# Where the later maxima of the keys are kept, and the join of two sets of them

## The chip, the cores and the metric

The kernel runs on one core of a Trainium2 chip. The metric is the device time of one execution in microseconds; smaller is better. Times of the kernel before are the median of three runs. The engines are named as in the profile: PE is TensorE (PEld its weight loads), DVE is VectorE, ACT is ScalarE, POOL is GpSimd, and SP is the engine whose queue issues the DMAs.

## The reference

One transformer block on `x` of 8 batches, 1024 tokens, 256 channels:

```
x = x + layernorm(attention(layernorm(x)))      # 16 heads of 64, causal, softmax
x = x + layernorm(channel_mix(layernorm(x)))    # sigmoid gate, squared ReLU, token shift

# attention, per batch and head
scores = (x Wq)(x Wk)^T / 8 + rel_table[clip(s - t + 16, 0, 32)]
scores = where(s <= t, scores, -inf)
out    = softmax(scores) (x Wv);   out @ Wp + bp
```

The softmax needs, for each query, a bound on its row of scores. The kernel takes the row's maximum of a cheaper product (high halves of q and k only), and the change concerns how those maxima are stored.

## The kernel before, in words

The work goes over 64 pairs of heads (8 batches of 8 pairs). One loop body works on one pair, and at the same time on parts of its neighbours: the projections of a pair two ahead, the maxima of the next pair, the second half of the pair before, and the output projection and channel mix of one block of 128 tokens of an earlier batch. Each engine has its instructions of a body in an order written out by hand; the engines meet at semaphores. There are two banks of PSUM for everything that is not scores (`misc`), two tiles of scores (`score_ps`) and one for the maxima (`max_ps`).

**The maxima.** For the next pair, PE fills `max_ps` nine times (`fill`, f from 0 to 8, L651 and, for the diagonal windows, L660). A query block i of 128 rows (8 in all) has either one reduction or, from i = 4 on, two: one over keys 0 to 511 (not diagonal) or part of them, and one that holds the diagonal. `FILLS` lists what a fill holds. After each fill, DVE reduces it (`maxima`, L1237 for fill 1, L1242 for the others) into `row_max`, a tile of 128 partitions and two planes of 128 floats. Columns in a group of 8 are (head of two, i modulo 4). In plane 0, columns 0 to 7 hold the maxima of the first four blocks, columns 8 to 15 the diagonal ones of the later four, columns 16 to 23 the others of the later four.

**The join.** `join_maxima` (L1249) waits until all nine fills are reduced, and then one reduction over the two groups of 8 in plane 0 writes the 8 final maxima of the later blocks to plane 1. PE transposes plane 0 after the fourth fill (`transpose_maxima`, L671) and plane 1 after the join, at the end of its body. ACT makes a row of shifts out of each transpose (`shift`, L959), and SP sends it to `shift_all`, from which PE adds it to the scores (L633).

**What stands around the join.** On DVE: the bias of tile 11 (`add_bias`, L1258), the join, the statistics of `y` (L1188, L1192), the bias of the next pair's tile 0, `low_probs` 11 (L1226). On PE: score 11, score 0 of the next pair, the transpose of plane 1, and then the next body: the value product of the channel mix (L743), fill 0, score 1, a product of probabilities and values (L694 to L696), the projections q0 and q1 (L585). On POOL, which has its own order: the normalisations (L382 to L399), the last step of the output rows (`final`, L1697), and the low halves of the probabilities for five of the twelve tiles (`low_probs`, L1670). Of these, tiles 8 and 10 come right after `final`. On SP: the rows of the output (L467, behind POOL's `final`), in every second body the values of two pairs (`v_pair`, L433), the store of a chunk (L444), the load of an `o_cur` block (L453), the load of the next `xh` (L463).

Of the kernel before, what the change touches and what calls it, by code (L numbers as in the profile page):

```python
# [35 lines left out]
ALU = mybir.AluOpType  # L36
ACT = mybir.ActivationFunctionType
AX = mybir.AxisListType
# [106 lines left out]
def build(nc, x, wqkv, wp, bp, table, w_r, w_k, w_v, mu_r, mu_k, out):  # L145
    with ExitStack() as ctx:
        def sb(name, shape, dt):
            return ctx.enter_context(nc.sbuf_tensor(name, shape, dt))
# [4 lines left out]
        def sem(name):  # L153
            return ctx.enter_context(nc.semaphore(name))
# [58 lines left out]


        row_max = sb("row_max", [P, 2, P], F32)
        later_max = row_max[:, 0, 8:24].rearrange("p (a h i) -> p a h i", a=2, h=2)
        shift_row = [sb(f"shift_row{c}", [8, P], F16) for c in range(2)]

        probs0 = sb("probs0", [P, 2, 2560], F16)
# [75 lines left out]
        max_ready = sem("max_ready")  # L295
# [36 lines left out]
        def wait(eng, semaphore, value):  # L332

            if isinstance(value, int) and value <= 0:
                return
            eng.wait_ge(semaphore, value)
# [843 lines left out]
        def _(dve):  # L1180
# [47 lines left out]
            def maxima(m, par, ahead, f):  # L1228

                n = 2 * m + par + ahead  # L1230
                dve.wait_ge(filled, NF * n + f + 1)
                if f == 0:
                    wait(dve, full["mt0"], n)
                    wait(dve, full["mt1"], n)
                if f == 1:
                    dst = row_max[:, 0, 0:32].rearrange("p (a b h i) -> p h a b i", a=2, b=2, h=2)[:, :, :, 0, 1:2]
                    last = dve.tensor_reduce(dst, max_ps[:].rearrange("p h (a w) -> p h a w", a=2), AX.X, ALU.max)  # L1237
                else:
                    for i, key, width, col, diagonal in FILLS[f]:
                        dst = (row_max[:, 0, 0:8].rearrange("p (h i) -> p h i", h=2) if i < 4  # L1240
                               else later_max[:, 0 if diagonal else 1])
                        last = dve.tensor_reduce(dst[:, :, i % 4:i % 4 + 1], max_ps[:, :, col:col + width], AX.X,  # L1242
                                                 ALU.max)
                last.then_inc(fill_used, 1)

            def join_maxima(m, par, ahead):
                n = 2 * m + par + ahead
                dve.wait_ge(fill_used, NF * (n + 1))
                dve.tensor_reduce(row_max[:, 1, 0:8], row_max[:, 0, 8:24].rearrange("p (a k) -> p k a", a=2), AX.X,  # L1249
                                  ALU.max).then_inc(max_ready, 1)  # L1250

            def add_bias(m, par, ahead, t, at):
                n = 2 * m + par + ahead
# [188 lines left out]
            for span in ALL_SPANS:  # L1442
                def body(m, par, at, span=span, has=span.has):
# [13 lines left out]
                    if has["next"]:  # L1457
                        maxima(m, par, 1, 0)
# [16 lines left out]
                    if has["next"]:  # L1475
                        maxima(m, par, 1, 1)
# [8 lines left out]
                    if has["next"]:  # L1485
                        maxima(m, par, 1, 2)
# [47 lines left out]
                    if has["next"]:  # L1534
                        join_maxima(m, par, 1)
# [257 lines left out]
```

## Time and profile before

| | |
|---|---|
| median of three runs | 2399.51 us (2395.8 to 2409.04) |
| profiled execution, its time | 2395.8 us |
| its span, first to last instruction | 2394.0 us |
| PE busy | 2221.1 us, 93% of the span |
| DVE busy | 2043.0 us, 85% |
| ACT busy | 1681.4 us, 70% |
| POOL busy | 1498.1 us, 63% |

Busy time is the union of an engine's instructions in the profile. Waits for semaphores, branches and the issuing of DMAs are not in it. Matmuls are pipelined and their ends are modelled, so PE's share is no measure of how near it is to its peak. A releaser is what an engine's idle time ended with, as the semaphores tell.

### The profile page before, as it was taken

The page shows a single profiled execution, that of the slowest core. Times are in us where ns is not written, and L with a number is a line of the kernel's source. Part 1 is how long each engine was busy: PE and PEld are TensorE (multiplying, and loading weights), DVE is VectorE, ACT ScalarE, POOL GpSimd, SP SyncE. Part 2 cuts the span into 40 slices and gives each one's busy share as a digit, 9 for nine tenths or more (in the row PEclk, how much of TensorE's full clock was granted, in tenths as well). Part 3 has the DMA queues.
Part 4 walks back from the last instruction along what each step waited for, and adds up shares of the span by engine and source line. Part 5 has one row for each costly group of instructions (what it writes and reads, how often), then busy time and mean ns, then how long its engine had stood idle before and what let it go on. Part 6 is the DMA issues. An engine that isn't in the chain of part 4 may idle for free.

```text
span 2394.0 us, 75663 instructions
## 1 busy us (share of the span) xinstructions
PE 2221.1 (93%) x30080; PEld 1486.8 (62%) x30080; DVE 2043.0 (85%) x3985; ACT 1681.4 (70%) x2526; POOL 1498.1 (63%) x2594
## 2 busy tenths in 40 slices
PE   3788889999999999999999999999999999999885
PEld 1455556666666666666666666666666666666664
DVE  6788878988888898888888988889898898988856
ACT  2577767777777776777777777777777777777743
POOL 2244335667776766767767777677677767565752
PEclk9999999999999999999999999999999999999997
DMA  6011111122122112212112211211221221121230
GB/s 166 28 41 42 40 48 51 39 68 64 52 65 64 57 42 68 62 50 68 55 39 68 64 57 59 64 57 42 68 63 50 67 62 52 40 64 59 62 108 21
DMA packets 182416, 139.81 MB, mean 58 GB/s; under 512 B 10416, under 2 KB 173104, under 8 KB 182064
## 3 DMA queue, kind: packets, MB, share of 16 engines
q1 hardware_dynamic: 182064, 134.98, 19.1%
q8 instruction: 238, 3.90, 0.7%
q14 instruction: 114, 0.93, 0.1%
HBM read 57.81 MB, written 43.06 MB: 42 GB/s over the span
## 4 chain that ended last, share of the span: by engine, by line
PE 77%; DVE 8%; DMA 6%; SPq 3%; ACT 3%; issue 2%; POOL 1%; DVEq 0%; POOLq 0%; ACTq 0%
PE score_ps L629 13%; PE misc L585 11%; PE misc L600 7%; PE max_ps L651 6%; PE misc L712 6%; PE misc L694 6%; DMA xh<-x 5%; PE misc L696 5%; PE misc L695 5%; PE score_ps L633 4%; PE misc L732 2%; PE misc L706 2%; PE misc L735 2%; PE max_ps L660 2%; DVE probs L1226 1%
## 5 line engine op out<-in xcount | busy, mean ns | idle before, releaser
L1670 POOL TENSOR_TENSOR probs<-probs_f,probs 128x1024 f16<-128x1024 f32 (+1 forms) x320 | 616.7, 1936 | 344.9 <-DVE x_mv L1192 194.5
L1242 DVE TENSOR_REDUCE row_max<-max_ps 128x2 f32<-128x1024 f32 (+2 forms) x640 | 633.0, 1006 | 29.9 <-PE max_ps L660 15.2
L977 ACT ACTIVATE score_ps<-score_ps,score_unit 128x1024 f32<-128x1024 f32 (+3 forms) x448 | 347.9, 777 | 197.9 <-DVE score_ps L1258 150.4
L694 PE MATMUL misc<-v_pair,probs 128*128 128x65 f16 x4608 | 445.3, 195 | 11.3 <-DVE q_lo L1201 7.8
L694 PEld LDWEIGHTS misc<-v_pair,probs 128*128 128x128 f16 x4608 | 418.9, 97 | 46.5 <-issue 36.7
L695 PE MATMUL misc<-v_pair,probs 128*128 128x64 f16 x4608 | 443.9, 194 | 0.0
L696 PE MATMUL misc<-v_pair,probs 128*128 128x65 f16 x4608 | 443.2, 194 | 0.0
L696 PEld LDWEIGHTS misc<-v_pair,probs 128*128 128x128 f16 x4608 | 421.5, 98 | 0.0
L695 PEld LDWEIGHTS misc<-v_pair,probs 128*128 128x128 f16 x4608 | 421.3, 98 | 0.0
L1226 DVE TENSOR_TENSOR probs<-score_ps,probs 128x1024 f16<-128x1024 f32 (+3 forms) x448 | 373.7, 834 | 46.1 <-ACT probs L995 43.4
L585 PE MATMUL misc<-xT,w_split 128*128 128x512 f16 x1536 | 369.6, 385 | 25.6 <-DVE o_stage L1270 16.5
L977 ACT ACTIVATE probs_f<-score_ps,score_unit 128x1024 f32<-128x1024 f32 (+1 forms) x320 | 328.1, 1025 | 54.1 <-PE score_ps L633 36.0
L995 ACT CAST probs<-score_ps 128x1024 f16<-128x1024 f32 (+3 forms) x448 | 317.3, 708 | 12.5
L995 ACT CAST probs<-probs_f 128x1024 f16<-128x1024 f32 (+1 forms) x320 | 307.3, 960 | 4.2
L629 PE MATMUL score_ps<-q_hi,k_hi 64*128 64x512 f16 (+3 forms) x1536 | 253.5, 325 | 37.0 <-DVE probs L1226 35.4
L1258 DVE TENSOR_TENSOR score_ps<-score_ps,bandT 128x288 f32<-128x288 f32 (+2 forms) x576 | 236.0, 420 | 44.5 <-PE score_ps L633 43.9
L585 PEld LDWEIGHTS misc<-xT,w_split 128*128 128x128 f16 x1536 | 140.7, 99 | 203.9 <-issue 44.1
L651 PE MATMUL max_ps<-k_hi,q_hi 64*128 64x512 f16 (+3 forms) x1536 | 225.4, 330 | 35.6 <-DVE row_max L1242 21.7
L633 PE MATMUL score_ps<-shift_all,shift_unit 64*128 64x512 f16 (+3 forms) x1536 | 252.2, 324 | 0.0
L629 PE MATMUL score_ps<-q_lo,k_hi 64*128 64x512 f16 (+3 forms) x1536 | 252.0, 323 | 0.0
L629 PE MATMUL score_ps<-q_hi,k_lo 64*128 64x512 f16 (+3 forms) x1536 | 252.0, 323 | 0.0
L600 PE MATMUL misc<-w_split,xT 128*128 128x256 f16 x1536 | 193.3, 277 | 0.0
(181 smaller groups left out, 4062.8 us busy)
## 6 DMA issues: line engine op xcount, KB each, us to landing
v_pair<-v_calc SPq DMA_DIRECT2D x64, 516.0 KB, 3.7
o_scratch<-o_stage SPq DMA_DIRECT2D x128, 256.0 KB, 2.5
o_cur<-o_scratch SPq DMA_DIRECT2D x56, 512.0 KB, 4.6
xh<-x SPq DMA_DIRECT2D x56, 128.0 KB, 4.1
x_res<-x SPq DMA_DIRECT2D x56, 128.0 KB, 2.1
out<-out_sb SPq DMA_DIRECT2D x56, 128.0 KB, 1.7
shift_all<-shift_row SPq DMA_DIRECT2D x256, 1.0 KB
probs<-wqkv SPq DMA_DIRECT2D x1, 3072.0 KB, 13.2
```

The costliest lines, as they stand in the source:

```text
L585: last = pe.matmul(bank[:], w_split[:, w, which, k, bass.ds(pair, P)], xT[:, a, k, bass.ds(ring + half * 512, 512)], start=step == 0, stop ...
L600: last = pe.matmul(bank[:, i * 2 * P:(i + 1) * 2 * P], xT[:, a, k, bass.ds(ring + (first + i) * P, P)], w_split[:, w, 2, k, bass.ds(pairs, ...
L629: pe.matmul(tile[:, h, 0:width], k_part[rows, ring, keys], q_part[rows, ring, cols], start=step == 0, stop=False)
L651: last = pe.matmul(max_ps[:, h, col:col + width], qk_hi[0][rows, ring, i * P:(i + 1) * P], qk_hi[1][rows, ring, key:key + width], start=Tr ...
L694: pe.matmul(bank[:, at:at + D + 1], high, v_high, start=j == 0, stop=False)
L695: pe.matmul(bank[:, at:at + D], high, v_low, start=False, stop=False)
L696: last = pe.matmul(bank[:, at:at + D + 1], low, v_high, start=False, stop=j == i)
L977: nc.scalar.activation(dst, score_ps[t % 2][:, :, 0:width], ACT.Exp, scale=score_unit[:]).then_inc(exp_done, 1)
L995: nc.scalar.copy(dst, src).then_inc(hi_done, 1)
L1226: dve.tensor_tensor(low, score_ps[t % 2][:, :, 0:width], high, ALU.subtract).then_inc(lo_done_dve, 1)
L1242: last = dve.tensor_reduce(dst[:, :, i % 4:i % 4 + 1], max_ps[:, :, col:col + width], AX.X, ALU.max)
L1670: pool.tensor_tensor(low, copy_of(par + ahead, t)[:, 0:2 * width], high, ALU.subtract).then_inc(lo_done_pool, 1)
```

## The change

The diagonal maxima of the later four blocks go straight to plane 1, columns 0 to 7. Those that are not diagonal go to columns 8 to 15 of plane 0. The join is an element-wise maximum of the two, written over the first of them, in place of a reduction over 16 columns. The waits and the place of each instruction in its engine's order are as before.

```diff
-        later_max = row_max[:, 0, 8:24].rearrange("p (a h i) -> p a h i", a=2, h=2)
+        row_max_a = row_max[:, 0, 8:16].rearrange("p (h i) -> p h i", h=2)
...
                 if f == 1:
-                    dst = row_max[:, 0, 0:32].rearrange("p (a b h i) -> p h a b i", a=2, b=2, h=2)[:, :, :, 0, 1:2]
+                    dst = row_max[:, 0, 0:16].rearrange("p (a h i) -> p h a i", a=2, h=2)[:, :, :, 1:2]
                     last = dve.tensor_reduce(dst, max_ps[:].rearrange("p h (a w) -> p h a w", a=2), AX.X, ALU.max)
                 else:
                     for i, key, width, col, diagonal in FILLS[f]:
-                        dst = (row_max[:, 0, 0:8].rearrange("p (h i) -> p h i", h=2) if i < 4
-                               else later_max[:, 0 if diagonal else 1])
+                        dst = (row_max[:, i // 4, 0:8].rearrange("p (h i) -> p h i", h=2) if diagonal
+                               else row_max_a)
...
             def join_maxima(m, par, ahead):
                 n = 2 * m + par + ahead
                 dve.wait_ge(fill_used, NF * (n + 1))
-                dve.tensor_reduce(row_max[:, 1, 0:8], row_max[:, 0, 8:24].rearrange("p (a k) -> p k a", a=2), AX.X,
-                                  ALU.max).then_inc(max_ready, 1)
+                both = row_max[:, 1, 0:8].rearrange("p (h i) -> p h i", h=2)
+                dve.tensor_tensor(both, both, row_max_a, ALU.max).then_inc(max_ready, 1)
```

## Rows read from the trace of the kernel before

**Rows 1.** The page, busy time by engine, and the chain that ended last.

```profile
PE 2221.1 (93%) x30080; PEld 1486.8 (62%) x30080; DVE 2043.0 (85%) x3985; ACT 1681.4 (70%) x2526; POOL 1498.1 (63%) x2594
...
PE 77%; DVE 8%; DMA 6%; SPq 3%; ACT 3%; issue 2%; POOL 1%; DVEq 0%; POOLq 0%; ACTq 0%
```

**Rows 2.** Stages: length; busy (instructions) of PE, PEld, DVE, ACT, POOL; clock; DMA share, GB/s.

```profile
1223.00:1257.00 34.00, 33.97 (x474) 22.89 (x472) 31.14 (x61) 25.85 (x40) 24.98 (x46) 1.00 0.15 44
1257.00:1293.00 36.00, 34.28 (x472) 22.78 (x470) 31.01 (x61) 25.71 (x40) 24.54 (x45) 1.00 0.24 72
```

**Rows 3.** Timeline around one join: start, us, engine, instruction, [idle <-releaser].

```profile
1222.70 3.25 POOL L1670 TENSOR_TENSOR probs<-probs_f,probs 128x1024 f16<-128x1024 f32 x2
...
1223.03 0.16 DVE L1249 TENSOR_REDUCE row_max<-row_max 128x8 f32<-128x16 f32 x1
...
1223.13 0.38 PE L633 MATMUL score_ps<-shift_all,shift_unit 64*128 64x512 f16 x2
...
1223.44 0.14 PEld L671 LDWEIGHTS max_ps<-ident,row_max 128*128 128x128 f32 x1 [0.42 <-DVE row_max L1249]
```

**Rows 4.** Timeline: five of the 64 joins, POOL's instruction beside three.

```profile
109.58 1.16 POOL L1670 TENSOR_TENSOR probs<-probs_f,probs 128x512 f16<-128x512 f32 x1 [1.49 <-ACT probs L995]
...
110.62 0.16 DVE L1249 TENSOR_REDUCE row_max<-row_max 128x8 f32<-128x16 f32 x1
...
444.85 2.14 POOL L1670 TENSOR_TENSOR probs<-probs_f,probs 128x1024 f16<-128x1024 f32 x1
...
445.20 0.16 DVE L1249 TENSOR_REDUCE row_max<-row_max 128x8 f32<-128x16 f32 x1
...
1257.09 0.16 DVE L1249 TENSOR_REDUCE row_max<-row_max 128x8 f32<-128x16 f32 x1
...
1293.28 0.16 DVE L1249 TENSOR_REDUCE row_max<-row_max 128x8 f32<-128x16 f32 x1
...
2264.02 2.13 POOL L1670 TENSOR_TENSOR probs<-probs_f,probs 128x1024 f16<-128x1024 f32 x1
...
2264.12 0.16 DVE L1249 TENSOR_REDUCE row_max<-row_max 128x8 f32<-128x16 f32 x1
```

**Rows 5.** Timeline of SP's queue and DVE behind the join at 1257 us.

```profile
1256.87 0.35 SPq L467 DMA_DIRECT2D out<-out_sb  x1
...
1263.71 0.42 DVE L1270 TENSOR_TENSOR o_stage<-misc,inv_sum 128x256 f32<-128x256 f32 x1 [1.61 <-DMA o_scratch<-o_stage]
1265.27 0.43 DVE L1188 BATCH_NORM_STATS2 xh_bn<-xh 128x6 f32<-128x256 f32 x1 [1.13 <-DMA xh<-x]
```

**Rows 6.** Waits by name over the run: total us, times, longest.

```profile
DVE xh_bn L1188 <- DMA xh<-x: 44.4, 30, 3.4
...
PEld max_ps L671 <- DVE row_max L1249: 37.6, 64, 1.7
...
DVE o_stage L1270 <- DMA o_scratch<-o_stage: 26.4, 28, 2.2
```

**Rows 7.** Groups by shape: count, busy us, mean ns, idle before, releasers.

```profile
L1670 POOL TENSOR_TENSOR probs<-probs_f,probs 128x1024 f16<-128x1024 f32 x256 | 544.9, 2130 | 326.7 <-DVE x_mv L1192 194.5 <-ACT probs L995 132.1
...
L1242 DVE TENSOR_REDUCE row_max<-max_ps 128x2 f32<-128x1024 f32 x384 | 467.7, 1218 | 16.8 <-PE max_ps L660 5.8 <-PE max_ps L651 4.6
...
L1226 DVE TENSOR_TENSOR probs<-score_ps,probs 128x1024 f16<-128x1024 f32 x128 | 156.1, 1220 | 36.6 <-ACT probs L995 36.5
...
L1249 DVE TENSOR_REDUCE row_max<-row_max 128x8 f32<-128x16 f32 x64 | 10.2, 160 | 0.0
...
L1580 DVE TENSOR_TENSOR xT<-xT 128x4 f32<-128x4 f32 x18 | 2.9, 163 | 0.6
```

**Rows 8.** Timeline of DVE and POOL in the last stretch.

```profile
2327.00 0.16 DVE L1580 TENSOR_TENSOR xT<-xT 128x4 f32<-128x4 f32 x1
...
2329.72 2.78 POOL L1746 TENSOR_TENSOR k_lo<-probs,q_lo 128x256 f32<-128x256 f32 x4 [12.38 <-ACT probs L1119]
```

**Rows 9.** The join's line: ns least/median/greatest, first to last start.

```profile
L1249 DVE TENSOR_REDUCE row_max<-row_max x64: 157/159/164, 78.6 to 2264.1; 128x8 f32<-128x16 f32 x64
```

## The prediction

> **What bounds the kernel now.** I read the page first. The parts by engine [rows 1] name TensorE (PE): busy 2221 of 2394 us, more than any other. VectorE (DVE) has 2043 us, 85%. The chain that ended last is PE for 77%, DVE for 8% and DMA for 6%. Any stall of PE between two matmuls is therefore paid, unless PE would have stood a little later anyway.
>
> The table by stage then sets two neighbouring pairs side by side [rows 2]. Between the joins at 1223 and 1257 us PE is busy for 33.97 of 34.00 us; between those at 1257 and 1293 us for 34.28 of 36.00 us. So there are two sorts of body. I call them tight (34.06 us from join to join, 1223.03 to 1257.09) and loose (36.19 us, 1257.09 to 1293.28) [rows 3, 4]. What makes the second loose is seen in DVE's timeline after 1261 us [rows 5]: its work on `o_stage` waits 1.61 us for the transfer `o_scratch<-o_stage`, then its statistics of `xh` wait 1.13 us for `xh<-x`. The waits by name say that this is regular: 30 waits of 44.4 us for `xh<-x`, 28 of 26.4 us for `o_scratch<-o_stage` [rows 6].
>
> Last I read what stands around the join (L1249). DVE starts it at 1223.03 and takes 0.16 us; PE's weight load for the transpose of the maxima (L671) starts at 1223.44 and has waited for the join alone, while the last matmuls of `score`, begun at 1223.13 and 0.38 us long, run out [rows 3]. Over the run this load waited 37.6 us for the join, in 64 waits [rows 6]. So the join is already as late as PE can bear: each microsecond that it gets later moves L671 and all that is queued behind it on PE (L743, the next pair's fill 0, its scores).
>
> **The change part by part.** *The maxima of the fills.* Nine fills a pair write the same number of maxima as before, with the same shapes; only the columns and the plane differ. Fill 1 keeps its one reduction to 128x4, with a destination stride of 8 floats where it was 16; the others keep theirs to 128x2, 1218 ns for 128x1024 [rows 7]. I take 0. Four of them now write plane 1, which the previous pair's second transpose reads. `maxima` already waits for both transposes of the previous pair at fill 0, so no wait is added, and no instruction, DMA or semaphore is moved.
>
> *The join, own time.* 64 reductions of 128x8 from 128x16, 160 ns each, become 64 `tensor_tensor` of 128x8 from twice 128x8. The nearest row is L1580, also a `tensor_tensor` with both inputs in SBUF, 128x4, 163 ns [rows 7]. That is 64 x 3 ns = 0.2 us more. Below, even a join of no length would give back only the 10.2 us of all 64 [rows 7].
>
> *The join, its company.* The reduction reads one operand from SBUF. The new instruction reads two. In the main loop DVE's two-operand instructions take one operand from PSUM (`score_ps` or `misc`, as L1270 and L1226 in [rows 5, 7]), and those run beside POOL without a mark. Those with two from SBUF stand in the first and the last stretch of the program, and POOL is idle beside them: L1580 and its neighbours from 2327.00 us, for one, while POOL's next work begins at 2329.72 [rows 8]. So the trace does not show such an instruction beside a POOL instruction. But that is what it meets: at 1223.03 POOL is 0.33 us into `low_probs` (L1670), which reads `probs_f` and `probs` from SBUF for 2.13 us [rows 3, 7]. I followed all 64 joins: in 53, from 445.20 us to the last at 2264.12 us, the same POOL instruction had started 0.03 to 0.35 us earlier and had 1.78 to 2.10 us left [rows 3, 4]; of the eleven before, seven met the last 0.12 us of the shorter one (as 110.62 against 109.58 + 1.16) and four nothing [rows 4].
>
> The cost is bounded on one side by no interplay (0.2 us in all) and on the other by waiting until POOL is done. What the rows show of POOL itself is that its two SBUF operands cost it dearly: 2130 ns for 1024 elements is 2.1 ns an element, where DVE takes 1.2 ns with one of its operands from SBUF (L1226, 1220 ns for 1024) [rows 7]. A POOL instruction that reads two operands thus looks bound by its reads, and a new reader of the same memory most likely meets it there. I take the wait, and of its two forms the one until the running instruction ends.
>
> The present join, with its one operand, is not held: 157 to 164 ns in all 64 [rows 9], POOL running beside 60 of them. The Trainium skill, page "SBUF — State Buffer", section "Who interferes with whom", says of this: a reduction never contends, while a VectorE instruction with both inputs in SBUF contends with a GpSimd instruction that reads SBUF, and whichever came second stands still until the first has ended. The trace agrees on the reduction and holds no case of the other. By that rule the change costs the waits that I sum below; without it, 0.2 us. It speaks plainly against the change.
>
> **The sum.** At 1223.03 the join would run from 1224.83 (1222.70 + 2.13) to about 1224.99, 1.80 us late. PE's transpose follows it by what it does now and starts 1.80 us late, and PE has nothing else: its queue is in order. DVE is late as well: the statistics of `y`, the bias of the next pair's tile 0, `low_probs` 11. POOL does not wait for those: it is busy with two `low_probs` until 1225.95 [rows 3].
>
> Tight bodies keep it all. Of the 53 delayed joins 29 open a body of under 34.7 us (or the last one): 29 x 1.89 us (mostly 1.80, ten of them 2.1) = 55 us.
>
> Loose bodies have cover: both transfers are issued in a queue that POOL's `out_sb` released at 1256.87, before the join, so that they land as early as now, and DVE, 1.80 us late, finds 1.61 + 1.13 us of its waiting gone [rows 5]. I take each body's cover as its length less 34.06 us and pay the rest. 24 loose bodies have covers of 0.9 to 4.7 us, 14 of them over 1.8; the others leave 0.3 to 0.9 us each, 6 us together. Seven early joins give 7 x 0.12 = 1 us. Sum: 55 + 6 + 1 = 62 us, with the 0.2 for the instruction itself lost in the rounding.
>
> The profiled execution took 2395.8 us with a span of 2394.0, 1.8 us outside it, and stands 3.7 us under the median of the runs, 2399.5. From its own time: 2395.8 + 62 = 2458; from the median, 2399.5 + 62 = 2462. I predict 2460 us, between the two.
>
> **The rivals.** *No interplay (not slower).* DVE reads both operands beside POOL as it now reads one. For it: the operands are 8 elements each, and no row of this trace shows DVE held by POOL. Against it: the reading rate of POOL above. It decides if the join lasts under 0.2 us while L1670 runs; 2399.5 + 0.2 = 2400 us.
>
> *The cover doesn't hold, or the queue goes against DVE.* If PE's own order, not the two transfers, sets the loose bodies once the join is late, all 53 waits are paid: 53 x 1.87 = 99 us, 2499 us. If DVE also loses the turn at 1224.83 to POOL's second `low_probs`, which follows without a gap and ends at 1225.95, a join is 2.92 us late: 29 x 2.9 = 84, and 23 from the loose bodies after their cover, 2508 us. For it: POOL's two instructions stand back to back [rows 3]. Against it: 1.72 us of PE's idle time in the loose stretch [rows 2].
>
> *The element-wise form is shorter (faster).* The nearest row speaks for 3 ns more, not less, and all 64 joins together are 10.2 us [rows 7]. Even if they were free, that would not reach 0.5%, about 12 us, which is what a measurement of this kernel can tell from no change.
>
> **How the numbers follow.** One wait with cover: 0.60, with its own range 2440 to 2480 us. Waits without cover or for two instructions: 0.19, 2480 to 2515. No interplay: 0.18, 2395 to 2410. Faster by something unseen: 0.03. Slower by over 0.5% is the sum of the first two, 0.79; the same 0.18; faster 0.03. A range for 8 in 10 can't leave out the case of no interplay, since the first two hold only 0.79: it goes from 2397 to 2506 us.
>
> **What would show it.** In the profile after: the join at 64 instructions with a mean near 1.7 us (its end at the end of POOL's first L1670), or its time as idle before it; the wait of PE's L671 for it near 37.6 + 98 = 135 us; the tight bodies at 35.9 us and the loose ones near 36.2; DVE's waits for `xh<-x` and `o_scratch<-o_stage` much under 44.4 and 26.4 us; POOL's L1670 unchanged at 2130 ns. A join of 160 to 170 ns with its start where it was would prove the main step wrong; a join that is late with the loose bodies at 38 us would prove the cover wrong.

## The result, and the profile after

The changed kernel takes 2430.87 us, the median of four runs (2426.18 to 2432.48), against 2397.99 us before in the same comparison. By the means of the runs, from which all ratios below are taken, that is 1.0125 times (1.009 to 1.016, the 95% interval that stands behind each ratio). It is slower by 33 us in the medians (30 in the means), by the mechanism that the prediction named, and by about half of what it summed: 62 us. The 2431 us lie between the prediction's two cases, 2395 to 2410 us for no interplay and 2440 to 2480 for its main one. The wide range of 2397 to 2506 us holds them only because it was stretched from the one over to the other. The profiled execution took 2431.3 us over a span of 2429.5, so 35.5 us more span than before.

The page gives the busy time of the engines and the chain that ended last:

```profile
PE 2216.6 (91%) x30080; PEld 1482.4 (61%) x30080; DVE 2128.2 (88%) x3985; ACT 1694.0 (70%) x2526; POOL 1499.2 (62%) x2594
...
PE 81%; DVE 10%; ACT 2%; DMA 2%; issue 2%; SPq 1%; POOL 1%; DVEq 0%; POOLq 0%; ACTq 0%
PE score_ps L629 13%; PE misc L585 13%; PE misc L600 7%; PE max_ps L651 7%; PE misc L694 6%; PE misc L712 6%; PE misc L695 5%; PE misc L696 5%; PE score_ps L633 4%; DVE row_max L1250 4%; PE misc L732 2%; PE misc L706 2%; PE misc L735 2%; PE
```

Against [rows 1], DVE is busy for 85 us more, and an instruction on 8 elements (L1250) has 4% of the chain. DMA has gone from 6% to 2% of it. Both halves of the result are in these two shares. The line of the join says the first (duration in ns, least, median, greatest; who waited for it, us and times):

```profile
L1250 DVE TENSOR_TENSOR row_max<-row_max x64: 156/1823/2130, 79.7 to 2299.1; 128x8 f32<-128x8 f32 x64
...
  PEld max_ps L671: 118.2, 64
  PE max_ps L671: 86.6, 63
```

In [rows 9] it was 157/159/164. Among the 64, the eleven before 445 us last 0.16 us still, as they meet POOL in its last 0.12 us or not at all. The next 52 last 1.79 to 2.13 us. The last one came when POOL had 0.80 us left and lasts 0.82. The timeline around one join, every engine:

```profile
1194.55 3.24 POOL L1670 TENSOR_TENSOR probs<-probs_f,probs 128x1024 f16<-128x1024 f32 x2
...
1194.88 1.82 DVE L1250 TENSOR_TENSOR row_max<-row_max 128x8 f32<-128x8 f32 x1
...
1194.98 0.38 PE L633 MATMUL score_ps<-shift_all,shift_unit 64*128 64x512 f16 x2
...
1196.75 0.14 PEld L671 LDWEIGHTS max_ps<-ident,row_max 128*128 128x128 f32 x1 [1.89 <-DVE row_max L1250]
1196.75 0.33 PE L671 MATMUL max_ps<-ident,row_max 128*128 128x128 f32 x1 [1.40 <-DVE row_max L1250]
1196.82 0.73 PEld L743 LDWEIGHTS misc<-wv_sb,k_act 128*128 128x128 f32 x4
```

The 3.24 us of POOL's row hold two instructions; the first takes 2.13 us (as it does alone, in a row further down) and so ends at 1196.68; the join ends at 1196.70; PE's transpose starts at 1196.75. POOL's pair of instructions takes 3.24 us, as in [rows 3] (3.25), so it is POOL that is served and DVE that stands. Beside [rows 3], note PE's own row: it now has 1.40 us of idle time. Before, L671 had none at the join of [rows 3]; only its weight load had waited. That holds for 54 of the 64 joins, as the view of the join's line in the kernel before says (who waited for it, us, times):

```profile
  PEld max_ps L671: 37.6, 64
  PE max_ps L671: 9.7, 10
```

The ten are the first ten joins; the trace shows 0.87 to 1.25 us of PE's own idle time at each.

The second half is in the table by stage (length; busy us of PE, PEld, DVE, ACT, POOL; clock; DMA share; GB/s) and in the waits:

```profile
1195.00:1230.50 35.50, 34.07 (x474) 22.87 (x470) 32.90 (x61) 26.15 (x40) 25.06 (x46) 1.00 0.25 73
1230.50:1266.00 35.50, 34.07 (x474) 22.89 (x470) 32.73 (x61) 26.14 (x40) 25.05 (x46) 1.00 0.14 43
```

```profile
DVE xh_bn L1188 <- DMA xh<-x: 17.2, 20, 2.3
```

These two, a loose one first, have become alike: 35.50 us. A tight body pays 1.44 us. A loose one, 36.19 us in [rows 4], is shorter than it was. Of the 21 loose bodies twelve are at 35.5 us now, the other nine at 35.7 to 37.2. The waits for `xh` fell from 44.4 us, and those for the store of `o_stage`, 26.4 us in [rows 6], to 1.3:

```profile
DVE o_stage L1270 <- DMA o_scratch<-o_stage: 1.3, 1, 1.3
```

The table sums the bodies over the whole trace, from join to join. The forecast is what the prediction's own rule gives from the trace of the kernel before, stretch by stretch:

| stretch | before | after | change | forecast |
|---|---|---|---|---|
| start, and the first 11 bodies | 445.2 | 445.6 | +0.4 | +0.8 |
| 21 tight bodies (numbers 11 to 51, odd) | 716.8 | 746.4 | +29.6 | +37.8 |
| 21 loose bodies (12 to 52, even) | 762.4 | 753.6 | -8.8 | +3.5 |
| the last 10 bodies and the end | 469.5 | 483.9 | +14.4 | +19.7 |
| span | 2394.0 | 2429.5 | +35.5 | +61.8 |

### The profile page after: what moved, and what is told of

The parts are those of the page before. It is cut to its first block, busy times and chain, and to the rows that moved or that the text cites. A ratio compares the mean times of both kernels' runs of the same rounds, so it can differ in the third digit from the quotient of the medians.

```text
span 2429.5 us, 75663 instructions
## 1 busy us (share of the span) xinstructions
PE 2216.6 (91%) x30080; PEld 1482.4 (61%) x30080; DVE 2128.2 (88%) x3985; ACT 1694.0 (70%) x2526; POOL 1499.2 (62%) x2594
## 4 chain that ended last, share of the span: by engine, by line
PE 81%; DVE 10%; ACT 2%; DMA 2%; issue 2%; SPq 1%; POOL 1%; DVEq 0%; POOLq 0%; ACTq 0%
PE score_ps L629 13%; PE misc L585 13%; PE misc L600 7%; PE max_ps L651 7%; PE misc L694 6%; PE misc L712 6%; PE misc L695 5%; PE misc L696 5%; PE score_ps L633 4%; DVE row_max L1250 4%; PE misc L732 2%; PE misc L706 2%; PE misc L735 2%; PE max_ps L660 2%; DMA xh<-x 2%
## 5 line engine op out<-in xcount | busy, mean ns | idle before, releaser
L977 ACT ACTIVATE probs_f<-score_ps,score_unit 128x1024 f32<-128x1024 f32 (+1 forms) x320 | 328.1, 1025 | 54.1 <-PE score_ps L633 35.8
L651 PE MATMUL max_ps<-k_hi,q_hi 64*128 64x512 f16 (+3 forms) x1536 | 225.9, 331 | 35.5 <-DVE row_max L1242 21.7
```

Of the source, the lines that this page charges most:

```text
L651: last = pe.matmul(max_ps[:, h, col:col + width], qk_hi[0][rows, ring, i * P:(i + 1) * P], qk_hi[1][rows, ring, key:key + width], start=Tr ...
L977: nc.scalar.activation(dst, score_ps[t % 2][:, :, 0:width], ACT.Exp, scale=score_unit[:]).then_inc(exp_done, 1)
```

## Experiments

**One instruction, before and after.** Does the second SBUF operand do it, or the new place of the maxima? Two kernels take the change apart. The first has the old layout and the new instruction:

```diff
-                dve.tensor_reduce(row_max[:, 1, 0:8], row_max[:, 0, 8:24].rearrange("p (a k) -> p k a", a=2), AX.X,
-                                  ALU.max).then_inc(max_ready, 1)
+                dve.tensor_tensor(row_max[:, 1, 0:8], row_max[:, 0, 8:16], row_max[:, 0, 16:24],
+                                  ALU.max).then_inc(max_ready, 1)
```

> The kernel before with the join alone changed: an element-wise maximum of columns 8 to 15 and 16 to 23 of plane 0, no plane 1 for the diagonal maxima. Theory (the second SBUF operand makes the join wait for POOL's running instruction): the 53 late joins last 1.8 to 2.1 us, their mean over 64 is near 1.58 us as in the kernel after, and the time is that of the kernel after, 2431 us (2426 to 2436). Rival (the writes of the reductions to plane 1, or the in-place output, cause the delay): joins of 0.16 us and 2398 us.

Measured: 2430.72 us, 1.0135 (1.0114 to 1.0157). The second has the new layout and a reduction over both planes (the diagonal maxima lie in columns 8 to 15 of plane 1 here, not 0 to 7, so that one reduction reaches both groups):

```diff
-                both = row_max[:, 1, 0:8].rearrange("p (h i) -> p h i", h=2)
-                dve.tensor_tensor(both, both, row_max_a, ALU.max).then_inc(max_ready, 1)
+                dve.tensor_reduce(row_max[:, 1, 0:8], row_max[:, :, 8:16].rearrange("p a k -> p k a"), AX.X,
+                                  ALU.max).then_inc(max_ready, 1)
...
-                        dst = (row_max[:, i // 4, 0:8].rearrange("p (h i) -> p h i", h=2) if diagonal
+                        first = 8 * (i // 4)
+                        dst = (row_max[:, i // 4, first:first + 8].rearrange("p (h i) -> p h i", h=2) if diagonal
```

> The kernel after with the join as a reduction again, over a group of 8 in each plane (one SBUF operand); the diagonal maxima stay in plane 1. Theory: joins of 0.16 us beside the same POOL instruction, 2398 us (2394 to 2403). Rival (the new place of the maxima costs): 2431 us, or part of the 33 us.

Measured: 2400.26 us, 1.0014 (0.9994 to 1.0035). The groups of the join by shape (count, busy us, mean ns, idle before), first of the kernel with the new instruction alone, then of the one with the new layout alone:

```profile
L1249 DVE TENSOR_TENSOR row_max<-row_max 128x8 f32<-128x8 f32 x64 | 102.0, 1594 | 0.0
```

```profile
L1250 DVE TENSOR_REDUCE row_max<-row_max 128x8 f32<-128x16 f32 x64 | 10.3, 160 | 0.0
```

The cost sits in the instruction. The layout shows none; by the interval it could be no more than 8 us.

**Who came first.** The wait needs POOL's instruction to have started. This kernel is the changed one, and POOL holds back until the join is done:

```diff
                     if has["att"]:
+                        if has["next"]:
+                            pool.wait_ge(max_ready, n + 2)
                         low_probs(m, par, 0, 8)
```

> The kernel after, with one wait added: POOL begins its low part of tile 8 only when the join of the same body is done. Theory (the join waits only because POOL's instruction came first): the join lasts 0.16 us in nearly all 64, POOL begins tile 8 about 0.55 us later than before, which nothing needs, and the time is 2398 us (2393 to 2405). If the operand from plane 1 or anything in the join itself were slow, the join stays near 1.8 us and the time at 2431 us or above.

Measured: 2404.27 us, 1.003 (1.0015 to 1.0045), so most of the 33 us are gone, and 8, clear of the noise, are left. The timeline of one join:

```profile
1230.57 0.16 DVE L1250 TENSOR_TENSOR row_max<-row_max 128x8 f32<-128x8 f32 x1
...
1230.80 2.13 POOL L1670 TENSOR_TENSOR probs<-probs_f,probs 128x1024 f16<-128x1024 f32 x1 [0.23 <-DVE row_max L1250]
...
1230.98 0.14 PEld L671 LDWEIGHTS max_ps<-ident,row_max 128*128 128x128 f32 x1 [0.42 <-DVE row_max L1250]
```

The same instruction on the same operands takes 0.16 us, 157 ns on the mean of 64. The time missed the middle of the expectation by 6 us: the tight bodies are at 34.06 us again, the loose ones sum to 768.5 us where they had 762.4, and the first eleven to 371.0 for 366.6. The layout-only kernel has 370.3 there as well, and the run with 128 no-operations, further down, 369.6, so 3 to 4 us there are what one execution differs from another; the 6 us in the loose bodies were not followed up.

**Until when it waits.** POOL's instruction for tile 8 cut in two:

```diff
+                src = copy_of(par + ahead, t)[:, 0:2 * width]
+                if t == 8:
+                    pool.tensor_tensor(low[:, 0:width], src[:, 0:width], high[:, 0:width], ALU.subtract)
+                    low, src, high = low[:, width:], src[:, width:], high[:, width:]
-                pool.tensor_tensor(low, copy_of(par + ahead, t)[:, 0:2 * width], high,
-                                   ALU.subtract).then_inc(lo_done_pool, 1)
+                pool.tensor_tensor(low, src, high, ALU.subtract).then_inc(lo_done_pool, 1)
```

> The kernel after, with POOL's low part of tile 8 in two instructions of 512 elements a partition each instead of one of 1024. Theory (the join waits for the POOL instruction that runs, and gets in before the next one): the join meets the first half 0.33 us after its start and ends with it, 0.83 us after the join's start; mean over 64 joins near 0.72 us, PE's transpose 0.5 us later than in the kernel before, tight bodies 34.55 us, time near 2410 us (2402 to 2418). Rival (it waits until POOL has nothing more to do, or loses the turn): joins of 1.9 us or more and 2431 us or above.

Measured: 2406.83 us, 1.0047 (1.003 to 1.0065), joins of 770 ns on the mean. DVE's and POOL's timelines:

```profile
1194.35 0.86 DVE L1250 TENSOR_TENSOR row_max<-row_max 128x8 f32<-128x8 f32 x1
...
1194.03 1.16 POOL L1672 TENSOR_TENSOR probs<-probs_f,probs 128x512 f16<-128x512 f32 x1
1195.14 2.27 POOL L1674 TENSOR_TENSOR probs<-probs_f,probs 128x512 f16<-128x512 f32 x2
```

The join ends at 1195.21, with the first half (1195.19), though POOL has three instructions back to back. It waits for the one that runs and not for the next, which the trace has from 1195.14 on. The rival of the prediction in which it loses the turn falls. Tight bodies are 34.53 us.

**How much lateness is free.** The kernel before with a dummy reduction ahead of the join. Its one operand comes from SBUF, and no reduction of that kind was held by POOL above. It writes a column that nothing reads:

```diff
+                dve.tensor_reduce(row_max[:, 1, 64:65], bandT[:].rearrange("p h j -> p (h j)")[:, 0:96], AX.X, ALU.max)
                 dve.tensor_reduce(row_max[:, 1, 0:8], row_max[:, 0, 8:24].rearrange("p (a k) -> p k a", a=2), AX.X,
                                   ALU.max).then_inc(max_ready, 1)
```

> The kernel before with a dummy reduction of 96 elements of the bias table in front of each join: the join 0.17 us later, no second SBUF operand. Theory (PE's transpose of the maxima is held by the end of score's matmuls until 0.41 us after the join's start, so that the join has 0.2 us to spare): tight bodies stay at 34.06 us, time 2396 to 2400 us. Rival (the prediction's step: each microsecond of lateness is paid): tight bodies 34.2 us, 64 x 0.17 = 11 us, 2407 us.

Measured: 2394.66 us, 0.9986 (0.9972 to 1.0). The dummy, the join, and the next join a tight body later in DVE's timeline, then what PE itself waited for the join over the run (total us, times, longest):

```profile
1222.17 0.24 DVE L1249 TENSOR_REDUCE row_max<-bandT 128x1 f32<-128x96 f32 x1
1222.33 0.16 DVE L1250 TENSOR_REDUCE row_max<-row_max 128x8 f32<-128x16 f32 x1
...
1256.38 0.16 DVE L1250 TENSOR_REDUCE row_max<-row_max 128x8 f32<-128x16 f32 x1
```

```profile
PE max_ps L671 <- DVE row_max L1250: 11.6, 10, 1.4
```

Tight bodies stay at 34.06 us. So a join 0.16 us later is free there, and the prediction's reading that it was "already as late as PE can bear" is refuted for them. It is right for the first ten joins alone, where PE's own wait grew from 9.7 to 11.6 us in all. The row in [rows 3] that led there is PEld's: "0.42 <-DVE row_max" counts the idle time of the weight load, in which PE's matmuls of `score` were still running. It is the same 0.42 in the run with POOL held back, above, in which PE itself has no gap either.

**The lateness alone.** The same kernel with 1536 elements in place of 96:

> The kernel before, its join a reduction, with a dummy reduction of 1536 elements of the bias table (one SBUF operand, some 1.75 us, 1.66 us from start to start) put in front of each join. It makes the join as late as the wait for POOL does, without POOL. Theory A (the cost of the change is the lateness of the join alone, and what the loose bodies win comes from the shifted phase): from the 12th body on as the kernel after, tight bodies 35.5 us and loose ones mostly 35.5 too; the eleven first bodies have the delay as well, at up to 1.4 us each, so 2431 + 12 = 2443 us (2436 to 2450). Theory B (POOL's hold of the memory has a further effect on transfers or engines): the loose bodies stay at 36 us or more and the time is over 2450 us.

Measured: 2454.19 us, 1.0233 (1.0211 to 1.0255). The dummy and the join, DVE's timeline:

```profile
1218.97 1.74 DVE L1249 TENSOR_REDUCE row_max<-bandT 128x1 f32<-128x1536 f32 x1
1220.63 0.16 DVE L1250 TENSOR_REDUCE row_max<-row_max 128x8 f32<-128x16 f32 x1
...
1254.47 1.74 DVE L1249 TENSOR_REDUCE row_max<-bandT 128x1 f32<-128x1536 f32 x1
1256.13 0.16 DVE L1250 TENSOR_REDUCE row_max<-row_max 128x8 f32<-128x16 f32 x1
```

Tight bodies are 35.50 us, and 14 of the 21 loose ones 35.5 or 35.6. From the 12th body on the stretches of the table above are 745.8, 755.3 and, for the last ten bodies without the end, 352.6 us; the changed kernel has 746.4, 753.6 and 353.5: theory A. The total is outside theory A's range, and over the 2450 us that theory B named, but not for theory B's reason: the loose bodies did not stay long. The first eleven bodies cost 24 us, twice what was expected, which is the whole miss of the total. Ten of them open with a join for which PE stood already, so they had no slack: PE's idle time there went from 0.87 us, in most, to 2.53, the whole 1.66 us of the lateness, some 17 us in ten bodies as an estimate. The mean granted clock was lower too, 0.93 of full speed against 0.98, and PE was busy for 337 us with the matmuls that had taken 322 (fields as in [rows 2], the kernel before first):

```profile
78.60:445.20 366.60, 321.70 (x4590) 205.38 (x4592) 303.34 (x531) 264.56 (x376) 161.06 (x206) 0.98 0.15 43
```

```profile
80.50:471.20 390.70, 337.39 (x4592) 217.41 (x4592) 321.61 (x543) 267.44 (x379) 162.84 (x206) 0.93 0.14 41
```

In these bodies the changed kernel has no wait, so that says nothing about it. The gain in the loose bodies thus needs no POOL either. It comes with the lateness of DVE and PE against the transfers; the waits for `xh` are down here too:

```profile
DVE xh_bn L1188 <- DMA xh<-x: 16.7, 18, 2.5
```

**The slack taken away.** In every second body the queue of SP sends `v_pair` (516 KB) before the store of `o_stage` and the load of `xh`, as in the kernel before at 1257 us:

```profile
1257.38 0.67 SPq L433 DMA_DIRECT2D v_pair<-v_calc  x1
1258.20 0.55 SPq L444 DMA_DIRECT2D o_scratch<-o_stage  x1
...
1260.07 0.81 SPq L463 DMA_DIRECT2D xh<-x  x1
```

In this kernel it goes behind them, in the next body:

```diff
                     if has["xt"] and (not isinstance(m, int) or n > -LEAD):
                         load_head(n + HEAD_LEAD)
+                    if par == 0 and runs("next", n - 1):
+                        load_values(m - 1, 1)
...
-                    if has["next"] and par == 1:
-                        load_values(m, par)
```

> The kernel before, with one transfer of every second body moved in SP's queue: the values of two pairs (v_pair, 516 KB) go behind the load of the next xh rather than in front of the store of o_stage. Theory (loose bodies are loose because the store and xh queue behind v_pair while the DMA engines are full): DVE's waits for xh and for the store nearly vanish, loose bodies 34.1 to 34.5 us, 21 x 2 us + 3 us less: 2350 us (2340 to 2365). Rival (what makes a loose body long is the sum of the bytes, or PE): the wait moves to the values (PE at the product of probabilities and values 0) and the time stays at 2385 us or above.

Measured: 2346.08 us, 0.9789 (0.9769 to 0.9809). SP's queue, then the table by stage of a body that was of the loose sort:

```profile
1163.18 0.38 SPq L444 DMA_DIRECT2D o_scratch<-o_stage  x1
1163.71 0.43 SPq L453 DMA_DIRECT2D o_cur<-o_scratch  x1
1164.24 0.39 SPq L463 DMA_DIRECT2D xh<-x  x1
1164.78 0.68 SPq L433 DMA_DIRECT2D v_pair<-v_calc  x1
```

```profile
1163.00:1197.00 34.00, 33.91 (x472) 22.93 (x470) 31.11 (x60) 25.72 (x39) 24.84 (x46) 1.00 0.26 76
```

PE is busy for 33.91 of 34.00 us there. The 21 loose bodies sum to 717.9 us, 44.5 less, and DVE's waits for `xh` are 8.1 us. Then the same edit on the changed kernel:

> The kernel after with the values' transfer moved behind the load of xh, as in the run before that took the slack out of the loose bodies (2346 us with the old join). Theory (the change costs 1.44 us in each body that has no slack, and the old order of the transfers hid or repaid it in every second body): all bodies from the 12th on are 35.5 us, 53 x 1.44 = 76 us more than 2346: 2420 us (2412 to 2428), 3.2% over its own base where the change cost 1.3% over its own. Rival (the join's wait is absorbed elsewhere in loose bodies, whatever the transfers do): 2346 + 33 = 2380 us.

Measured: 2419.12 us, 1.0086 times the kernel before (1.0069 to 1.0103). Its joins:

```profile
1186.32 1.80 DVE L1250 TENSOR_TENSOR row_max<-row_max 128x8 f32<-128x8 f32 x1
...
1221.80 1.79 DVE L1250 TENSOR_TENSOR row_max<-row_max 128x8 f32<-128x8 f32 x1
...
1257.27 1.79 DVE L1250 TENSOR_TENSOR row_max<-row_max 128x8 f32<-128x8 f32 x1
```

All bodies are 35.47 or 35.48 us, or 35.7 to 35.8 where the join's wait is the longer one of 2.1 us. On this base the change costs 2419.12 - 2346.08 = 73 us, 3.1%, where on the given base it costs 33. (The kernel before took 2395.85 us beside the one median and 2398.85 beside the other; against the version with both, below, measured beside this one, it is 71.) So some 40 us of the cost had been hidden or paid back by bodies that waited for transfers.

**The version with both.** The changed kernel with the values later and POOL behind the join:

> The kernel after with the values' transfer moved and with POOL's low part of tile 8 behind the join. Theory (with POOL out of its way the element-wise join is as good as the reduction, and the slack is gone): joins of 0.16 us, bodies 34.06 us, 2347 us (2343 to 2353), 2.1% under the kernel before. Rival (the added wait on POOL costs something that the loose bodies hid): 2355 us or more.

Measured: 2347.67 us, 0.9789 (0.9774 to 0.9803), joins of 157 ns. It equals the kernel before with the values later, 2346.08 us. Both beat both kernels by 50 and 83 us, and neither owes anything to the element-wise join.

**Why `xh` lands earlier: not settled.** In the loose bodies of the kernel before, `xh` lands 7.06 to 9.11 us after the join's start. The DMA records show instructions coming in by packets of 16 KB, 238 in the run, in a queue of their own, each at the median 1.0 us of one DMA engine. The records do not say whose they are. We take them for PE's code, an inference from shares: PE and its weight loads have 80% of the instructions that the page counts (60160 of 75663), this queue has 3.90 of the 4.83 MB of both instruction queues. Two loose bodies, seen in the DMA view from 1.0 to 6.3 us after their joins at 1257.09 and 1748.75 (queue: packets, MB, share; transfers: count, KB, us to landing):

```profile
q8 instruction: 1, 0.02, 1.1%
...
xh<-x SPq DMA_DIRECT2D x1, 128.0 KB, 5.1
```

```profile
q1 hardware_dynamic: 1826, 1.41, 88.4%
...
xh<-x SPq DMA_DIRECT2D x1, 128.0 KB, 4.1
```

The first has a code packet, the second none. Counted so over the 21 loose bodies of five executions whose joins are not late (before, layout only, POOL waits, little late, and the first shift below), 61 have a packet in that stretch and `xh` lands at 8.32 us on the mean; 44 have none, and it lands at 7.37. In the changed kernel the packet comes later in the body, 6.2 us or more after the join's start where it was 4.1 or more: 1 of 21 bodies has it in the stretch, and the mean landing is 7.55 us against 8.02 before. Against the packets speaks that four bodies of the changed kernel without one in the stretch have `xh` landing at 8.63 to 9.05 us, later than the mean of those with one. Two kernels tried to move the packets. The first puts 128 no-operations before PE's first transpose:

```diff
+            for _ in range(128):
+                pe.nop(nofuse=True)
             pe.wait_ge(ident_ready, 1)
```

> The kernel before with 128 PE no-operations in front of its first transpose, which POOL's and DVE's set-up hides. They move the points at which PE's code is fetched (16 KB packets, 238 in the run) by half a packet against the program. Theory (a loose body of the kernel before is 36.3 us where a code packet falls among its transfers and 35.3 us where it comes after them): the alternation swaps, so that bodies 14, 18, 22, 36, 40, 44 and 48, 35.2 to 35.5 us now, become 36 us or more, and bodies 12, 16, 20, 26, 30, 34, 38 and 42, 36.2 to 36.7 us now, mostly 35.1 to 35.5 us; the time changes by less than 10 us. Rival (something else, such as the state of the DRAM or of the rings, sets the landing): the same bodies stay long, or no pattern.

Measured: 2395.88 us, 1.0003 (0.9989 to 1.0018). The number of packets stayed at 238. Against the joins their times stayed where they were, but for two bodies, 26 and 52, and the long bodies stayed long, these two apart. The second uses real instructions:

```diff
                 transpose_heads(g)
+            for _ in range(64):
+                pe.matmul(max_ps[:, 0, 0:2], ident[:], ident[:, 0:2], start=True, stop=True)
```

> The kernel before with 64 dummy matmuls of two columns (128 instructions with their weight loads) in PE's idle stretch at 27 to 33 us, in place of the no-operations that left the code packets where they were. Theory (a PE code packet among the transfers of a loose body makes xh land a microsecond later): the packets' times move, and the long ones among the loose bodies are again those with a packet 1.0 to 6.3 us after the join's start, xh landing at 8.3 us in them against 7.4 us in the others; if the shift is half a packet, bodies 14, 18, 22, 36, 40, 44, 48 become the long ones. Total within 10 us of 2396 us. Rival: the packets move and the same bodies stay long.

Measured: 2418.71 us, 1.0088 (1.0064 to 1.0111), outside the expected 10 us. The 20 us are these matmuls themselves, which overran the idle stretch (27.3 us in PE's timeline); the first join came at 97.3 us for 78.6, and the bodies after it have the old lengths. There is one packet more, and within the loose bodies they lie where they lay, but for bodies 26 and 52 again. So neither kernel moved what it should, and the test was never made. Bodies 26 and 52 come nearest to it. In the profiled execution of the kernel before they have a packet 4.08 and 4.28 us after the join's start, and `xh` lands at 8.17 and 7.94 us. In five others (layout only, POOL waits, little late, and the two shifts) the first packet of these bodies comes at 10.4 us or later, and `xh` lands at 6.66 to 7.36 us. That fits the packets, but no edit brought it about, and what moved the packets there is not known. That they delay `xh` remains an association over a few executions, not shown.

## Why the prediction was off by half

**The mechanism** was right in its main steps: the join meets POOL's running instruction in 53 bodies, waits until that one ends, PE's transpose follows, POOL is not slowed. The rules of the Trainium skill, page "SBUF — State Buffer", section "Who interferes with whom", hold here on two points. The join with two SBUF inputs stands behind a POOL instruction that reads SBUF (1.82 us); the reduction never does (160 ns). On the third, that who comes first decides, the runs show half: with POOL's instruction behind it the join is not held (157 ns). POOL waited at a semaphore there, so no run shows a POOL instruction held by the join. The prediction's own reason, that POOL looks bound by its reads, was not tested. The rival of no interplay is out, and so is the one in which the loose bodies pay all: they got shorter.

**The term of the tight bodies** was too large by a fifth: 1.80 us forecast, 1.44 measured. 0.14 us went because the join's own 0.16 us do not come on top of the wait: it ends 0.02 us after POOL, so it is 1.66 us late, not 1.80. 0.20 us were PE's to spare: its load of L671 could not start before 0.41 us after the join's start (1223.44 - 1223.03 in [rows 3]), while the join, done at 0.16, lets it start at 0.21, by the 0.05 us between 1196.70 and 1196.75 after. 1.80 - 0.14 - 0.20 = 1.46. The step that failed is "each microsecond that it gets later moves L671". It read the idle time of the weight load as PE's. Beside the forecasts of the table this mis-sizing is 8 us in the tight bodies, most of the 5 us in the last ten and the end, and 2 us in the loose ones, where 3.5 us were to be left and 1.44 us against their covers leave 1.1. The 0.12 us each of the seven early joins fell away too: a join that starts that near to the end of POOL's instruction lasts 0.16 us, as before. The time that the weight load L671 waited for the join, which the prediction put near 135 us, is 118.2.

**The cover** held in its place, and more came back than was asked. The prediction took the landing of the transfers as fixed, so a loose body could be no shorter than before. By that and 1.44 us the 21 loose bodies would have gone from 762.4 to 763.5 us. They went to 753.6. `xh` lands 0.47 us earlier on the mean, although SP issues each transfer at the same time after the join as before (`xh` 2.98 us after: 1197.86 - 1194.88, and 1260.07 - 1257.09 in the kernel before). Body by body the traces tell what that is worth. In the kernel before, 19 of the 21 loose bodies last 28.14 us more than the landing of `xh` after their join, to 0.01 us; in the changed kernel they do so, to 0.04 us, where that is over 35.5 us, and else last 35.5 us (up to 0.3 more where the join's wait is the longer one). By this the earlier landing is worth 7 us. The other 3 us are bodies 24 and 32, which were 1.5 and 1.7 us longer than their landing made them and are so no more; what had held them was not followed up. That is the second step that failed: "they land as early as now". The runs show that the lateness brings it about (with a dummy in place of POOL the loose bodies sum to 755.3 us). What in the lateness does so stays open.

The two together: 62 us forecast in the table, less 16 for the size of the wait, less 10 in the loose bodies, is 36; the span grew by 35.5.

## What to carry to other kernels

Before a VectorE instruction gets a second SBUF operand, look up what GpSimd runs at that time: here the price was the rest of GpSimd's instruction, up to 2.1 us for an instruction on 8 elements, and splitting that instruction or issuing it behind lowered it. To price lateness on TensorE, read the matmul's row, not the weight load's, and subtract what the matmuls before it still cover. And where every second body waits for transfers, a local cost can be hidden there: here 33 us showed of 73. Look at such waits first: here removing them was worth 50 us, more than the join could ever have been.

## What the runs showed of the hardware that had not been expected

An 8-element `tensor_tensor` that waits 1.8 us for POOL ends 0.02 us after POOL's instruction, 1196.70 against 1196.68: its own 0.16 us do not come on top of the wait. That is so at all 53 late joins (0.02 us at each). A packet of 16 KB in the instruction queue keeps one DMA engine for 1.0 us at the median, and the packets' places in nearly all bodies did not move when 128 instructions were put in front of them.
